# A click-through ranking kernel whose dynamic-DMA scratch goes from 16 KB to 8 KB per SBUF partition

## The reference

```
e = stack([tbl_f[ids[:, f]] for f in range(39)], axis=1)      # 2048 x 39 x 16
x0 = xk = e
for W, b in layers:                                            # three, 128 outputs each
    z = relu(einsum('bhd,bkd,hks->bsd', x0, xk, W) + b)
    xk, direct = z[:, :64], z[:, 64:]                          # the last layer is all direct
h = concatenate([sum_d(direct of all layers), dense_ctx])      # 256 + 16
y = relu(relu(h @ W_top1 + b_top1) @ W_top2 + b_top2) @ W_top3
```

## Time and profile before

| | |
|---|---|
| time, median of 3 executions | 2473.49 us (2471.82 to 2473.76) |
| time of the profiled execution | 2473.12 us |
| its span | 2471.3 us (1.8 us lie around it) |
| PE busy (matmuls) | 2417.4 us, 98% |
| DVE busy | 2224.4 us, 90% |
| POOL busy | 1948.2 us, 79%: L414 448 times, L408 624 times |
| ACT busy | 1733.9 us, 70% |
| chain that ended last | PE 57%, POOL 25%, issue 13%, DVE 3% |
| mean granted clock of TensorE | 0.993 of full speed |
| DMA | 16 engines, sync engine's queue q1 65.2% of their time, POOL's queue q0 2.4% |

### The profile page before, as it was taken

How to read it: one execution, slowest core, us unless ns; L and a number is a source line. 1 busy time by engine, 2 the same in 40 slices (tenths; PEclk the granted TensorE clock), 3 DMA queues, 4 the chain that set the end, 5 groups by cost and what they waited for, 6 DMA issues and landing times.

```text
span 2471.3 us, 33379 instructions
## 1 busy us (share of the span) xinstructions
PE 2417.4 (98%) x8886; PEld 1646.7 (67%) x8886; DVE 2224.4 (90%) x1894; ACT 1733.9 (70%) x2203; POOL 1948.2 (79%) x1331
## 2 busy tenths in 40 slices
PE   5899999999999999999999999999999999999989
PEld 2566666666666666666666666666666666666656
DVE  1599999999989999999999999899999999999993
ACT  1677777777767777767777776677777777777655
POOL 6688888888878888888888888788888888866550
PEclk9899999999999999999999999999999999999999
DMA  3778667766856866776786677586677667667730
GB/s 75 156 146 175 140 137 163 154 140 143 174 121 143 172 136 139 165 154 137 147 169 138 139 166 152 115 171 146 137 154 165 138 136 173 146 136 153 164 92 1
DMA packets 214717, 352.61 MB, mean 143 GB/s; under 512 B 34382, under 2 KB 47566, under 8 KB 214588
## 3 DMA queue, kind: packets, MB, share of 16 engines
q1 hardware_dynamic: 194717, 347.07, 65.2%
q0 software_dynamic: 19968, 5.15, 2.4%
HBM read 346.97 MB, written 5.12 MB: 142 GB/s over the span
## 4 chain that ended last, share of the span: by engine, by line
PE 57%; POOL 25%; issue 13%; DVE 3%; ACT 1%; POOLq 0%; DMA 0%; ACTq 0%; DVEq 0%
PE ps L897 21%; PE ps L907 11%; POOL Pl L414 11%; PE ps L887 10%; POOL emb L408 10%; PE ps L875 8%; PE ps L870 3%; POOL dir L443 2%; DVE ps L752 1%; DVE P L752 1%; DVE Pl L757 1%; POOL sqx L420 1%; PE ps L1014 1%; PE ps L863 1%; PE ps L1024 1%
## 5 line engine op out<-in xcount | busy, mean ns | idle before, releaser
L414 POOL TENSOR_TENSOR Pl<-P,Ph 128x1024 fp32r<-128x1024 f32 x448 | 1074.6, 2399 | 285.9 <-ACT Ph L558 260.7
L897 PE MATMUL ps<-Ph,wh 128*128 128x512 f32 x2048 | 965.1, 471 | 9.7 <-ACT Ph L558 9.7
L558 ACT ACTIVATE Ph<-ps 128x1024 fp32r<-128x1024 f32 x576 | 590.3, 1025 | 405.9 <-DVE ps L752 394.3
L752 DVE TENSOR_TENSOR P<-xb,ps 128x1024 f32<-128x1024 f32 x704 | 854.5, 1214 | 3.2 <-DMA xb<-x_dram 3.2
L757 DVE TENSOR_TENSOR Pl<-ps,Ph 128x1024 fp32r<-128x1024 f32 x576 | 705.4, 1225 | 113.5 <-ACT Ph L558 94.7
L897 PE MATMUL ps<-Ph,wl 128*128 128x512 f32 x1920 | 755.3, 393 | 0.0
L907 PE MATMUL ps<-Pl,wh 128*128 128x512 f32 x2048 | 741.9, 443 | 8.2 <-POOL Pl L414 8.2
L408 POOL DMA_INDIRECT emb<-tbl_in,idx x624 | 600.4, 962 | 171.4 <-issue 146.0
L752 DVE TENSOR_TENSOR ps<-xb,ps 128x1024 f32<-128x1024 f32 x576 | 706.9, 1227 | 30.3 <-issue 10.2
L558 ACT ACTIVATE Ph<-P 128x1024 fp32r<-128x1024 f32 x448 | 473.9, 1058 | 186.5 <-DVE P L752 120.5
L907 PEld LDWEIGHTS ps<-Pl,wh 128*128 128x128 f32 x2048 | 384.2, 188 | 200.9 <-issue 118.1
(11 more groups left out here) (84 smaller groups left out, 893.7 us busy)
## 6 DMA issues: line engine op xcount, KB each, us to landing
xb<-x_dram SPq DMA_DIRECT2D x1280, 256.0 KB
emb<-tbl_in,idx POOLq DMA_INDIRECT x624
x_dram<-rows SPq DMA_DIRECT2D x64, 78.0 KB
xb<-w_in SPq DMA_DIRECT2D x16, 128.0 KB
xb<-wt_in SPq DMA_DIRECT2D x2, 512.0 KB, 4.3
xb<-dense_in SPq DMA_DIRECT2D x1, 768.0 KB, 5.3
wp<-w_in SPq DMA_DIRECT2D x4, 128.0 KB
xb<-w0a_in SPq DMA_DIRECT2D x1, 448.0 KB
```

The lines of the kernel that those rows point to most:

```text
L414: pool.tensor_tensor(Pl[:, h_slot(ref, c, k)], P[:, p_slot(ref, c, k)], Ph[:, h_slot(ref, c, k)], ALU.subtract).then_inc(low_pool, 1)
L558: act.activation(Ph[:, h_slot(ref, c, k)], p, ACT.Copy).then_inc(rounded, 1)
L752: dve.tensor_tensor(p, xb[:, x], xk.unsqueeze(1).broadcast_to([128, 2, N]), ALU.mult)\
L897: pe.matmul(z_of(c, k), w[:, q, j, :], Ph[:, h_slot(ref, c, k), j, :], start=k in (L1B, L2) and i + j == 0, stop=False)
```

## The change

The size of the dynamic DMA scratch is given as 8192 bytes per partition in place of the default of 16384. The instructions, their order and their waits stay the same; the tensors begin 8 KB lower in each partition.

```diff
-    nc = bacc.Bacc("TRN2", target_bir_lowering=False, num_devices=1)
+    nc = bacc.Bacc("TRN2", target_bir_lowering=False, num_devices=1, dynamic_dma_scratch_size=8192)
```

## The result

| | before | after |
|---|---|---|
| time, median | 2473.06 us | 2481.27 us |
| lowest, highest | 2471.3, 2474.37 | 2479.44, 2482.95 |
| profiled execution, its span | 2473.12, 2471.3 | 2479.44, 2477.5 |

The ratio is 1.0032 (95% interval 1.0021 to 1.0044): 8.2 us slower by the medians, 6.3 between the two profiled executions. The forecast was 2485.8, 12.7 slower, with a range of 2472 to 2496.

The account below looks back on a forecast made before the run. PE sets the pace and POOL can make it late, waiting at lap ends of its DMA ring. New stalls 3 x 5.8 + 2.9 + 1.8 + 2.9 = 25.0, less 12.3, give +12.7 on 2473.12: 2485.8 us, range 2472 to 2496.

Parts of the forecast that it names:

- Some 2.1 to 2.8 us more: At a lap's end POOL waits until all its DMAs have landed, then 2.1 to 2.8 us before the next gather.
- the heavy ones: Lap ends behind 168, 224 and 616 gathers, amid heavy q1 broadcast traffic: 5.8 us each.
- behind 392: Lap end with quiet DMA engines and no reserve before POOL's next low part: 2.9 us.
- Behind 336 and 560: Lap ends with 1.1 us of POOL reserve: 2.9 late costs 1.8 behind 336, 4.0 late costs 2.9 behind 560.
- The clock: Behind PE's wait at a heavy place the granted clock falls to 0.50, losing 1.7 us; no fall at shorter waits.
- the place behind 224: Lap end whose forerunner's landing wasn't told apart from its neighbours': between 1.8 and 5.8 us, taken as 5.8.
- 12.3 taken away: Old stalls behind 226 and 565 gathers vanish with the 16384-byte laps: 5.8 + 6.5 us saved.
- Behind 56, 112, 280, 448 and 504: Lap ends costing nothing: 56 covered by POOL's wait for ACT, 448 cancels an old stall, the others by a low part.
- Nothing changes: Rival, chance 0.09: the stalls aren't laps of the scratch; 2473.1 us, 2471 to 2475.
- The stall shrinks with the ring: Rival, chance 0.07: going back to the ring's start costs time in proportion to its size; faster, 2465 us.
- Only the part behind the landing halves: Rival, chance 0.04: PE waits 1.2 us less at each of six places, its clock never falls; 2473.5 us.
- The clock falls everywhere: Rival, chance 0.10: upward clock bounds together, plus a PE wait recurring in the next steps; 2491 to 2500, say 2494 us.

Follow-up runs that it names:

- light8k: Kernel after (8192 bytes) with the tile loop's sync-engine broadcasts carrying 128 of the 512 columns: 2464.32 us in one run.
- pad8k: Kernel after with an unused tensor of 8192 bytes per partition allocated first, putting other tensors back where they lay before: 2484.05 us, ratio 1.0039 to before.
- ring16896: Kernel after with a scratch of 16896 bytes, nothing else: 2479.63 us, ratio 1.0031 to before.
- ring5632: Kernel after with a scratch of 5632 bytes, nothing else: 2471.03 us, ratio 0.9993 to before.
- ring11264: Kernel after with a scratch of 11264 bytes, nothing else: 2473.09 us, ratio 0.9998 to before.
- ring5504: Kernel after with a scratch of 5504 bytes, nothing else: 2492.76 us, ratio 1.0080 to before.
- shift3: Kernel after plus three unused prologue gathers reporting to their own semaphore; scratch 5632, 11264 or 16384 bytes: 2458.95, 2460.16, 2473.05 us.
- shift1: Kernel after with 5632 bytes of scratch and one extra prologue gather reporting to its own semaphore: 2458.89 us in one run.
- sem5632: Kernel after with 5632 bytes of scratch, no extra gather, the 57th gather reporting to its own semaphore: 2460.72 us, ratio 0.9949 to before.

## Why the prediction was right, and where its sizes were off

- **The mechanism.** Laps of 113 and 56 gathers, a wait for landings at each end, PE caught by it where POOL has little reserve: as forecast, shown by the places in the profile after, by the laps of 78, 39, 38 and 117, and by light8k. That addresses cost nothing is shown by pad8k. The 16 bytes of a descriptor in the Trainium skill ("DMA: Bandwidth & Descriptors", section "Terms") fit all of them: 344, 352, 512, 704 and 1056 descriptors divided by nine are 38.2, 39.1, 56.9, 78.2 and 117.3, and the laps are 38, 39, 56, 78 and 117 gathers. That the stalls are not VectorE's doing is shown by the series of sizes: their places move with the ring while VectorE's work stays. For a VectorE instruction with two SBUF inputs the Trainium skill ("SBUF — State Buffer", section "SBUF: two separate sides") limits the lock to a GpSimd instruction that reads SBUF, which the prediction left out.
- **"Some 2.1 to 2.8 us more" behind the landing** was taken as a constant. It is not: in quiet places the next gather starts 2.1 us behind the landing with 16384 bytes (3.18 idle, of which 1.07 to the landing), 1.5 with 8192 (2.73, of which 1.2) and 1.3 with 5504 (2.44, of which 1.15). The prediction had named another time than 2.1 to 2.8 us as a sign of being wrong, and in this step it was. My evidence, all from one size, couldn't tell a constant from a share of the ring. It made four places too dear: PE's waits of 4.08 us in the heavy ones measured 3.42, 3.47 and 3.64, and behind 392 POOL stood idle 2.73 us where 3.2 were forecast. Behind 336 and 560 it took nothing off: POOL stood idle 3.46 and 4.11 us there, where 3.2 and about 4.3 were forecast.
- **The clock.** 1.7 us for each heavy place, 5.1 in all. It fell at two of the three; 3.4 us at most. That it fell at no wait of 1.8 us was in the forecast as the lower choice and held; in ring16896 it fell at each of the five waits of 2.2 to 2.3 us.
- **The sum.** What a place costs is read from its turn, since a wait in the profile is counted from the modelled end of the matmul before it. These are the turns in which 336, 392 and 560 lie, the last stretch of the kernel after, with 616 in it, and the same stretch of the kernel before:

```profile
1046.28:1192.18 145.90, 144.48 (x537) 98.97 (x536) 136.99 (x117) 105.64 (x135) 121.63 (x83) 1.00 0.71 149
1336.34:1482.71 146.37, 144.52 (x537) 98.97 (x536) 136.96 (x117) 105.61 (x135) 121.66 (x83) 1.00 0.71 148
1915.28:2061.46 146.18, 144.47 (x537) 99.02 (x536) 136.99 (x117) 105.63 (x135) 121.62 (x83) 1.00 0.71 148
2061.46:2477.50 416.04, 399.07 (x1481) 274.26 (x1479) 352.78 (x306) 278.93 (x356) 241.94 (x145) 0.99 0.54 117
...
2060.48:2471.30 410.82, 397.07 (x1481) 272.93 (x1479) 352.77 (x306) 278.71 (x356) 241.99 (x145) 1.00 0.54 118
```

| behind | forecast | measured |
|---|---|---|
| 168 | 5.8 | 5.3 |
| 224 | 5.8 | 3.8 |
| 616 | 5.8 | 5.2 |
| 392 | 2.9 | 2.2 |
| 336 | 1.8 | 1.7 |
| 560 | 2.9 | 2.0 |
| together | 25.0 | 20.2 |

The largest miss is the place behind 224, for which the prediction had nothing better than a value between 1.8 and 5.8 and took the upper end; the clock that didn't fall there is 1.7 of its 2.0. With 12.3 taken away the net is 7.9. The start of the program, before the first place that counts, took 1.3 off (the gather behind 78 starts at 171.45 in place of 172.79, with a shorter stretch of low clock ahead of it), which leaves 6.6 where the profiled executions differ by 6.3. Whether the other executions start like that, and so why the medians differ by 8.2, isn't shown. The range of 2472 to 2496 reached over no change, so the time alone says little for the working; the places of the stalls say more.
- **Behind 56, 112, 280, 448 and 504**: costed at nothing, and no wait of PE over 0.3 us stands there. Behind 56 POOL stood idle 7.7 us and PE 0.3.
- **The rivals.** "Nothing changes" is out. "The stall shrinks with the ring" was half true: a part of it does, but the wait for landings doesn't, and there are more of them. "Only the part behind the landing halves" had the right part but too much of it: from 16384 to 8192 bytes it went from 2.1 to 1.5 us in quiet places, and the clock did fall at two waits. "The clock falls everywhere" is out, as it fell at two of the six. Over all laps the going over comes to about the same for every size (15 x 1.02 us with 5632 bytes, 7 x 1.93 with 11264), which is why ring5632 and ring11264 ended within 2.1 us of each other. That they also ended near the kernel before is a coincidence: what they saved in waits for landings, 12.3 us, they paid, fully exposed, in going over the ring behind the copy of the indices.
- **Open.** What POOL does in the time that grows with the ring, and why it costs 2.6 ns for 16 bytes behind the copy of the indices and 1.2 behind a landing. A low part that stands directly ahead of the gather seems to cover it: behind 339 gathers in the kernel before, 504 in the kernel after, 168 and 616 in light8k and 456 in ring5504 the idle time is 0.14 to 0.17 us. In the two of light8k and behind 504 the gather starts 2.6 us after its forerunner's end, as it does behind 392 in light8k without a low part, so nothing was left to do behind the low part. The run made to move a lap's end there on purpose moved it elsewhere. Also open is why the clock fell at some waits of PE of 2.1 to 3.5 us and not at others.

## What to carry to other kernels

Where an engine issues many small DMAs through a ring, look for a stall with a period in the count of DMAs rather than in the loop, and divide the ring's bytes by that count. Its cost is set by what lands late when the lap ends and by what is queued behind it, so choose the ring so that laps end in a quiet place that recurs (here a lap equal to one turn of the loop), and fix the phase; here the size alone cost up to 0.8%, and a lap in the right place took 0.5% off.

## What the runs showed of the hardware

A gather that reports to another semaphore than the one before it starts a new lap of the ring (laps counted from 60, 58 and 57 gathers in shift3, shift1 and sem5632), though the ring is not full by then (18 gathers into a lap of 39, 57 into one of 78 or of 113). The change of semaphore was tried at this one point of the program, in the prologue. And a lap's end costs time that grows with the ring even if nothing is in flight: 1.02, 1.93 and 2.84 us at 5632, 11264 and 16896 bytes behind the copy of the indices, 2.6 ns for each 16 bytes. In quiet places behind a landing the growth is 1.2 ns for each 16 bytes (idle 2.37, 2.59, 2.86 and 3.18 us at 5632, 8192, 11264 and 16384 bytes).
